# Two relation layers of a graph network: one-hot picking products in float32r on a table split in two parts

## What is computed

```python
def rgcn_conv(x, src, dst, edge_type, W, root, bias):
    x_src = x[src]
    for r in range(8):
        msg = msg + where(edge_type == r, x_src @ W[r], 0)
    cnt = zeros((nodes, 8)).at[dst, edge_type].add(1.0)
    norm = 1.0 / maximum(cnt[dst, edge_type], 1.0)
    agg = segment_sum(msg * norm, dst)
    return agg + x @ root + bias
```

## Time and profile before

| | us |
|---|---|
| median of 3 runs | 18148.49 |
| lowest and highest run | 18147.04, 18175.33 |
| span of the profiled execution | 18161.1 |

### The profile page before, as it was taken

The page is one execution under the profiler, slowest core; times in us unless marked ns, Lnnn a source line. Parts: engine busy times, 40 slices in busy tenths (PEclk is TensorE's granted clock), DMA queues, the critical chain, the costliest instruction groups (busy, mean ns, idle before and its releaser), DMA issues. The chain is left out here.

```text
span 18161.1 us, 349411 instructions
## 1 busy us (share of the span) xinstructions
PE 15098.9 (83%) x83251; PEld 13315.7 (73%) x83252; DVE 14620.2 (81%) x36172; ACT 11849.6 (65%) x23181; POOL 10508.1 (58%) x29948
## 2 busy tenths in 40 slices
PE   0148847998998999899699998999969999499997
PEld 0048846887887888789688885777747777399996
DVE  4745557887887888788699997999958888499997
ACT  2000026777777777678577777888858888377775
POOL 0458836775775775777477765666622424376610
PEclk9555558999999999999899999999989999699998
DMA  7611121010000100000211112222211212111111
GB/s 233 125 26 40 40 78 27 23 24 22 23 24 22 24 24 23 23 24 24 34 31 31 31 25 65 73 71 72 74 43 61 67 61 67 33 31 31 30 27 17
DMA packets 1268447, 826.81 MB, mean 46 GB/s; under 512 B 873458, under 2 KB 1213398, under 8 KB 1260758
## 3 DMA queue, kind: packets, MB, share of 16 engines
q1 hardware_dynamic: 880918, 671.78, 13.2%
q0 software_dynamic: 269056, 117.80, 3.5%
q10 hardware_dynamic: 118080, 33.61, 1.0%
HBM read 587.33 MB, written 235.06 MB: 45 GB/s over the span
## 5 line engine op out<-in xcount | busy, mean ns | idle before, releaser
L1548 PE MATMUL powers_sums<-powers_b_hot,powers_spread 128*128 128x224 f32 x26400 | 5284.7, 361 | 670.8 <-DVE powers_b_hot L1529 455.7
L1548 PEld LDWEIGHTS powers_sums<-powers_b_hot,powers_spread 128*128 128x128 f32 x26400 | 5097.4, 195 | 860.3 <-issue 826.7
L1650 POOL DMA_INDIRECT filled<-powers_by_b,powers_at_start x2688 | 3364.3, 1252 | 1721.6 <-issue 847.3
L2351 PE MATMUL relate_got<-relate_hot,relate_table 112*128 112x512 f32 (+1 forms) x10560 | 3091.5, 435 | 110.8 <-ACT relate_hot L2313 70.5
L1543 ACT ACTIVATE powers_b_hot<-powers_away,ones 128x672 f32<-128x672 f32 x2640 | 1977.9, 751 | 1251.6 <-PE powers_sums L1548 880.1
L1537 ACT ACTIVATE powers_away<-wide,powers_minus_b 128x224 f32<-128x224 f32 x6600 | 2717.6, 472 | 117.5 <-ACT powers_minus_b L1718 35.0
L2351 PEld LDWEIGHTS relate_got<-relate_hot,relate_table 112*128 112x128 f32 x10560 | 1702.7, 191 | 1388.5 <-issue 1315.0
L1526 DVE TENSOR_TENSOR powers_spread<-powers_a_hot,powers_message 128x640 f32<-128x640 f32 x2640 | 2154.4, 816 | 517.5 <-PE powers_sums L1548 327.8
L2313 ACT ACTIVATE relate_hot<-relate_away,ones 112x1280 f32<-112x1280 bf16 x1320 | 1797.9, 1362 | 734.3 <-PE relate_got L2351 447.3
L1529 DVE TENSOR_SCALAR powers_b_hot<-wide,powers_b_val 128x224 f32<-128x224 f32 x6600 | 1918.5, 339 | 0.0
L2366 PE MATMUL relate_mixed<-relate_mix,relate_picked 128*128 128x128 f32 x13200 | 1711.4, 277 | 107.3 <-issue 92.2
(11 more groups left out here) (475 smaller groups left out, 25622.2 us busy)
## 6 DMA issues: line engine op xcount, KB each, us to landing
relate_codes<-pair_rows SPq DMA_DIRECT2D x264, 800.0 KB
powers_given<-filled SPq DMA_DIRECT2D x528, 200.0 KB
rec<-relate_running SPq DMA_DIRECT2D x132, 400.0 KB
filled<-powers_by_b,powers_at_start POOLq DMA_INDIRECT x2688
grouped<-order_blanks POOLq DMA_DIRECT2D x20, 1320.0 KB
filled<-order_blanks SPq DMA_DIRECT2D x20, 1320.0 KB
held_recs<-grouped SPq DMA_DIRECT2D x132, 200.0 KB
conv_given<-filled SPq DMA_DIRECT2D x132, 200.0 KB
```

What stands on the lines that cost most here:

```text
L1548: mm = pe.matmul(gathering.sums[:, bass.ds(group * STRIDE, WINDOW)], spread[:, j].rearrange("p a d -> p (a d)"), b_hot[:, j, :], start=Fal ...
L1650: pool.indirect_dma_start(filled, bass.IndirectOffsetOnAxis(to, 0), rows, None).then_inc(spread_out[block % 2], 16)
L2351: mm = pe.matmul(got[:, n % 2, at:to], table[:, n // SLOTS % 2, half, :], flat[:, at:to], start=half == 0, stop=half == 1, skip_group_chec ...
```

## The change

The node table is kept in two parts. After the table's rows have landed in `by_b`, DVE rounds them into `upper` (type float32r, twelve bits) and subtracts that from the original into `under`, once per layer; the two steps are in DVE's list ahead of its first `kinds_of`. ACT now waits for these (semaphore `halved`) and not for the DMA alone. At the first unit of a turn ACT makes two copies into a `table` of twice the size, of `under` and of `by_b`, both rounded to float32r on the way. `hot` is a float32r tile. `gather` runs twice as many products, all of them float32r: for each half and each of the two parts, pieces of 512 and 128 columns into the same sums in `got`.

```diff
-        hot = s.sb("hot", [HALF, HOTS, 2, TILES, P])
+        hot = s.sb("hot", [HALF, HOTS, 2, TILES, P], F32R)
...
-        table = s.sb("table", [HALF, 2, 2, 8 * D])
+        upper = s.sb("upper", [HALF, 2 * GROUPS, 8 * D], F32R)
+        under = s.sb("under", [HALF, 2 * GROUPS, 8 * D])
+        table = s.sb("table", [HALF, 2, 2, 2, 8 * D], F32R)
...
-                    act.copy(table[:, k % 2], by_b[:, bass.ds(group * 2, 2), :]).then_inc(tabled, 1)
+                    act.copy(table[:, k % 2, 0], under[:, bass.ds(group * 2, 2), :])
+                    act.copy(table[:, k % 2, 1], by_b[:, bass.ds(group * 2, 2), :]).then_inc(tabled, 1)
...
-            act.wait_ge(table_in, 16)
+            act.wait_ge(halved, 2)
...
-                    for at in range(0, WIDE, PIECE):
-                        to = min(at + PIECE, WIDE)
-                        mm = pe.matmul(got[:, n % 2, at:to], table[:, n // SLOTS % 2, half, :],
-                                       flat[:, at:to], start=half == 0, stop=half == 1, skip_group_check=True)
+                    for part in range(2):
+                        for at in range(0, WIDE, PIECE):
+                            to = min(at + PIECE, WIDE)
+                            mm = pe.matmul(got[:, n % 2, at:to], table[:, n // SLOTS % 2, part, half, :],
+                                           flat[:, at:to], start=half == part == 0, stop=half == part == 1,
+                                           skip_group_check=True)
...
+            dve.wait_ge(table_in, 16)
+            dve.tensor_copy(upper[:], by_b[:]).then_inc(halved, 1)
+            dve.wait_ge(halved, 1)
+            dve.tensor_tensor(under[:], by_b[:], upper[:].bitcast(F32), ALU.subtract).then_inc(halved, 1)
             kinds_of(0, True)
```

More of the change, by code:

```diff
@@ L6 @@
 F32 = mybir.dt.float32
+F32R = mybir.dt.float32r
 BF16 = mybir.dt.bfloat16
@@ L2198, in relation_sums @@
         codes_in, through_in = s.sems("codes_in", G_RING), s.sems("through_in", 2)
-        (set_up, weights_in, mix_ready, y_out, table_in, tabled, measured, hotted, gathered, selected, made, weighed, reduced, scanned,
+        (set_up, weights_in, mix_ready, y_out, table_in, halved, tabled, measured, hotted, gathered, selected, made, weighed, reduced, scanned,
          lasted, carried, backed, lifted, repaired, stored, kinds, shared, ends_in, added, gate, gate_act, gate_pe, loading) = (
              s.sem(n) for n in (
-                 "set_up", "weights_in", "mix_ready", "y_out", "table_in", "tabled", "measured", "hotted", "gathered", "selected", "made",
+                 "set_up", "weights_in", "mix_ready", "y_out", "table_in", "halved", "tabled", "measured", "hotted", "gathered", "selected", "made",
                  "weighed", "reduced", "scanned", "lasted", "carried", "backed", "lifted", "repaired", "stored", "kinds", "shared",
```

## The result

| | before | after |
|---|---|---|
| median of the runs, us | 18147.76 | 17891.52 |
| lowest and highest, us | 18143.08, 18175.33 | 17875.13, 17920.19 |
| span of the profiled execution, us | 18161.1 | 17889.0 |

The ratio of after to before is 0.9858, with a 95% interval of 0.9844 to 0.9872: 256 us less by the medians, 272 by the two profiled executions, of which before's lies high. The forecast was 17847, the range 17740 to 17990. The time lies 44 us above the forecast, but the parts came out otherwise than the sum had them: of 302 us, the first layer was to give 67 and gave none, the second was to give 235 and gave 282.

A forecast was written before the change was run, and what follows sets the result against it. PE was taken to bound both layers' loops. Gains of 67 us (first layer) and 235 (second) sum to 302 off the profiled 18161.1, giving 17859, or 17847 off the median; range 17740 to 17990.

The forecast's parts named there:

- The bound and the picking products: PE bounds both loops at 33.43 us a pair; float32r products priced near bf16's cut the gather from 2.17 us.
- The term of 1.31: Gather time in us after the change: 4 x 0.217 for 512-column products plus 4 x 0.11 for load-and-product pairs.
- (b): Rival: float32r column costs half of f32's, or products still run as f32; PE stays bound, about 18155 us; chance 0.10.
- (c): Rival: each float32r product costs as much as an f32 one; gather 4.34 us, total 20900; chance 0.07.
- What is late next: With PE at 24.8 us a pair, DVE paces the first layer's loop at 31, ACT the second's at 29.6.
- The second layer: Loop gains 245 us, less 6 for stalls and 4 for the split at the start: 235 us gained.
- The 6 us for stalls at POOL's additions: Second-layer loss from DVE stalling at POOL's six additions, which PE absorbs before the change; between 0 and 18 us.
- left alone: The 190 us from the second layer's last store to its end, mostly engines waiting for instructions, assumed unchanged.
- The first layer: The loop alone would gain 155 us, but POOL's end caps the layer's gain at 67 us.
- POOL's chain doesn't move: First layer: nothing in POOL's work but its last 10.44 us waits for the loop, so POOL would end at 13283.8.
- the 67 us of slack: First-layer gain until POOL ends the layer: add_nodes at about 13286 where it was 13352.9.
- Rival (d): PE, now idle a fifth of each pair, drops to its 1.2 GHz clock; 19750 us in full, chance 0.08.

The follow-up runs named there:

- e1: Changed kernel without the products of the table's lower part, half of the gather's products; first layer 2394.6 us, second 2108.4, second-layer pair 29.28.
- e5: Changed kernel with half of DVE's scans of one line left out in both layers; first layer 2382.7 us, second 2119.8.
- e2: Changed kernel with split and second copies kept, but f32 products of one part; first layer 2385.9 us, second 2399.8, second-layer pair 33.48.
- e7: Changed kernel with pauses also among POOL's indirect DMAs of each layer's last collecting group; first layer 2405.5 us, second 2116.1.
- e6: Changed kernel with POOL collecting only two of the seven groups in the first layer; first layer 2206.2 us, second 2114.9.
- e3: Kernel before, with ten more two-input DVE additions a pair in the first layer; first layer 2385.9 us, POOL's first part 1510.5.
- e4: Kernel before, with ten more one-input DVE reductions a pair in the first layer; first layer 2388.6 us, POOL's first part 1495.6.
- e9: Changed kernel, first layer's sixth group without pauses, second layer's last group with pauses in its first 40 gathers; ratio to before 0.9778.

## Why the prediction came out as it did

**The bound and the picking products: right.** PE fell off the bound, and the lower price was the true one: one record a product, 1.41 us a gather, between the bounds of 1.09 and 1.97. The term of 1.31, four bf16 pitches and four pitches of a load with its product, was 0.10 too small. It cost nothing, as the text said of any gather up to 1.8; e1 shows it. Rivals (b) and (c) fell with the same row. That twelve bits are the reason, as the text had it, no run shows; the rows show one record a product.

**What is late next: right.** DVE in the first layer, 31.0 forecast and 30.93 measured; ACT in the second, 29.6 forecast and 29.30 measured. e5 shows both: without half of DVE's scans the first layer's pair fell to 29.73 and the second's stayed at 29.29. The 0.3 is the unit, 2.87 in the text and 2.84 in the rows, ten of them 28.4; the 0.9 us for the four copies was right: 28.4 + 0.9 = 29.3.

**The second layer: right in its mechanism, 47 us too small.** The loop's 62 pairs gave 259.9 us where 63 pairs at 3.89 were to give 245: the pace (62 x 0.30 = 18 us). The 6 us for stalls at POOL's additions didn't show: 28.4 + 0.9 is the whole pair. The start, from `add_nodes` to the first store, is 7.8 us shorter (117.5 against 125.3), where 4 us for the split were to come off one pair's 3.9; e2 has the split at 2.7 there by itself. The rest behind the last store, "left alone", is 14 us shorter. That step left 190 us unexamined: e7 puts 114 of after's 176 down to one cause.

**The first layer: the step that failed.** "POOL's chain doesn't move" took POOL's durations as fixed because its waits didn't hang on the loop. Its durations changed. The cap was right (e6), the 67 us of slack were right (the table), and no store wait showed in any group, as was forecast; but POOL's indirect DMAs grew by 72 us. The text named the mechanism and gave it at most 25 us, worked out from seven additions (there are six); the additions kept their 3.5 us, and the indirect DMAs, 652 of the spreading in this layer's lines and 98 of each group, are what grew (POOL issues more of the program's DMAs than SP does, 8338 against 3644). Some 68 of the 72 lie in those beside a two-input DVE instruction: 476 x (1152 - 952) ns = 95 us against 510 x (1003 - 949) ns = 28. The text saw a busier DVE slow POOL's gathers "nowhere", but before's trace had it: 65 DMAs over 1.1 us, all beside such an instruction, and a longest gather of 1615 ns beside a median of 943. e3 and e4 show a fuller DVE to be enough for the first part. How much of it comes in the collecting isn't settled: e7 and e9 show that the same loop can leave the groups at 177 to 187 us.

The 90 us by which DVE was to be done before POOL came out as 296. Of the 206 more, 72 are POOL's growth and 125 the last round, which fell ahead of POOL's unpaused group and took 63 us for 188. It cost nothing, as POOL was the end.

**Rival (d), the clock: there, and free.** In the first layer PE stands once a pair for DVE, and its next products run at a lower clock. PE's timeline, first layer:

```profile
12007.17 0.26 PE L2388 MATMUL relate_mixed<-ident,relate_carried_in 16*128 16x16 f32 x2 [2.27 <-DVE relate_picked L2421]
12007.36 1.50 PE L2372 MATMUL relate_mixed<-relate_mix,relate_picked 128*128 128x128 f32 x10
12008.51 2.80 PE L2356 MATMUL relate_got<-relate_hot,relate_table 112*128 112x512 f32 x8
```

And two windows of it, these five us and fifteen behind them (the 0.66 and the 1.00 are the granted clock):

```profile
12007.40:12012.40 5.00, 5.00 (x27) 4.61 (x27) 5.00 (x8) 3.54 (x4) 3.31 (x13) 0.66 0.02 4
12015.00:12030.00 15.00, 14.16 (x98) 12.43 (x98) 14.62 (x34) 14.71 (x18) 10.20 (x50) 1.00 0.45 153
```

Behind 2.27 us of standing still a gather takes 2.80 where it takes 1.56: part of these five us is at the 1.2 GHz level, and further on it is 2.4 again. The stretch as a whole has 0.95. In four stretches of 500 us from 11000 on it is 0.93, 0.95, 0.94 and 0.99, so that the text's sign of this rival, under 0.95, was there in two of them; in the second layer it is 1.00, as the text had it. It cost nothing, because PE had the time to spare, and the rival as priced left that out: a tenth of the time at the low level was to cost 105 us, while the pair stayed DVE's.

**The sum.** 302 forecast, 272 measured: -72 for the first layer, +47 for the second, -4.4 for stages that the change doesn't touch. Two errors of opposite sign made the total look better than its parts; that it lies so near the forecast is luck.

## What to carry to other kernels

When a bound moves, an engine that waits for nobody is not thereby constant: see whether its own instructions slow down under the engine that will now be full, and price it over all of its instructions, not over those that a row happens to show. Look in the trace of before for a longest duration far from the median, and at what runs beside it. Where POOL issues DMAs without pause, other engines can stand still; look for long idle times on "issue" beside it, and put the unpaused stretch where the others are idle. Before a change of type is costed to the last tenth, ask from which price on it matters; here half of the products gave the same pairs.

## What the runs showed of the hardware

- A float32r product is one record where f32 has two, and 2560 columns of it took 1.41 us with eight weight loads, against 2.17 for 1280 columns of f32.
- POOL's indirect DMAs are held up by DVE instructions with two SBUF inputs, and more of them when DVE is fuller: in after 182 of the 476 beside one took over 1.1 us, mean 1152 ns, and 1 of the 862 others, mean 952. Ten added DVE instructions a pair cost 20 to 34 us over the first part of POOL's chain.
- POOL's indirect DMAs without pauses hold up the other engines, which stand on "issue": 176 us for a written-out round that takes 62 with pauses; and with half the pauses a loop of 31 us a pair took 45.
- With the pauses half as long the loop took 33.15 us a pair: their length counts, not only their number.
